# A graph layer's edge loop rebuilt: tiles of 128 edges, one f32 product per tile, bias moved into the node table, a ring of 26 row tiles

## The reference

```python
xn  = layernorm(x)                                    # 1250 x 512
msg = relu(xn[src] + edge_attr @ W_e + b_e)           # 21250 x 512
aggr = segment_sum(msg, dst, 1250)                    # summed by destination
h = (1 + eps) * xn + aggr
h = silu(batchnorm(h @ W1 + b1)); y = silu(batchnorm(h @ W2 + b2))
x = x + y                                             # then layernorm, top-k, experts
```

## Time and profile before

| | us |
|---|---|
| median of the three timed runs | 633.88 |
| span of the profiled execution, first to last instruction | 659.6 |
| first gather issued | 26.95 |
| last gather issued | 300.38 |
| last sum added to `aggT` (edge loop done) | 328.56 |
| expert stage begins (PE dense) | about 505 |

### The profile page before, as it was taken

One profiled execution on the slowest core, in us unless ns is written; L12 is line 12 of the kernel. 1 busy time (PEld: TensorE's weight loads), 2 busy tenths in 40 slices (PEclk: granted clock), 3 DMA queues, 4 the chain that ended last, 5 costly groups with the idle time before them and its releaser, 6 DMA issues.

```text
span 659.6 us, 12121 instructions
## 1 busy us (share of the span) xinstructions
PE 515.8 (78%) x4075; PEld 368.6 (56%) x4075; DVE 410.4 (62%) x1056; ACT 362.9 (55%) x754; POOL 304.4 (46%) x249
## 2 busy tenths in 40 slices
PE   3458678887868987978799996670279999999990
PEld 2324334554434553545445653550179999999990
DVE  7557676764554665766557963668666766766530
ACT  3527667654553555656648613843306667667760
POOL 3377887878777666772000000000054465555531
PEclk9979988997897988999989998785559999999996
DMA  9799866667766666663346730781027999994322
GB/s 240 221 227 208 206 177 181 181 185 188 183 187 176 162 160 163 174 176 98 118 139 233 186 120 0 218 286 63 0 60 232 280 293 283 283 280 82 59 32 28
DMA packets 76088, 111.59 MB, mean 169 GB/s; under 512 B 32201, under 2 KB 36865, under 8 KB 76027
## 3 DMA queue, kind: packets, MB, share of 16 engines
q0 software_dynamic: 43712, 53.95, 33.7%
q1 hardware_dynamic: 32211, 56.70, 28.5%
q10 hardware_dynamic: 104, 0.17, 0.1%
HBM read 97.81 MB, written 12.79 MB: 168 GB/s over the span
## 4 chain that ended last, share of the span: by engine, by line
PE 58%; issue 11%; DVE 11%; ACT 10%; DMA 4%; another core or an unknown queue 2%; POOL 1%; DVEq 1%; ACTq 1%; POOLq 0%; SPq 0%
PE bank L1365 19%; PE bank L1549 11%; PE bank L1342 10%; ACT big L612 4%; PE bank L1356 3%; DVE bank L995 3%; PE bank L1358 3%; PE bank L1575 2%; DMA big<-node_rows,edge_home 2%; PE bank L1412 1%; PE bank L1539 1%; PE bank L1530 1%; DVE rows_z L1172 1%; PE bank L1418 1%
## 5 line engine op out<-in xcount | busy, mean ns | idle before, releaser
L1342 PE MATMUL bank<-big,edge_home 125*64 125x256 f32 x688 | 99.0, 421 | 49.9 <-ACT big L612 34.1
L477 POOL DMA_INDIRECT big<-node_rows,edge_home x90 | 111.9, 1244 | 54.9 <-issue 47.7
L487 POOL DMA_INDIRECT big<-token_rows,idx x32 | 36.6, 1143 | 215.3 <-DVE idx L1230 209.8
L477 POOL DMA_INDIRECT pair<-node_rows,edge_home x80 | 99.4, 1243 | 29.3 <-issue 22.6
L612 ACT ACTIVATE big<-bank 125x512 f32<-125x512 f32 x170 | 96.0, 594 | 30.1 <-DVE bank L995 22.9
L1365 PE MATMUL bank<-big,pair 128*128 128x156 f16 (+2 forms) x1056 | 106.5, 260 | 1.1 <-DVE big L1050 0.9
L1342 PEld LDWEIGHTS bank<-big,edge_home 125*64 125x64 f32 x688 | 46.5, 146 | 92.2 <-ACT big L612 47.1
L1365 PEld LDWEIGHTS bank<-big,pair 128*128 128x128 f16 x1056 | 80.9, 97 | 24.6 <-issue 1.4
L1356 PE MATMUL bank<-edge_home 128*125 128x512 f16 x172 | 71.4, 415 | 6.0 <-issue 6.0
L995 DVE SCALAR_TENSOR_TENSOR bank<-big,bank 125x512 f32<-125x512 f32 x90 | 59.1, 708 | 26.7 <-PE bank L1358 14.2
L496 POOL DMA_INDIRECT out<-rows_z,idx x32 | 51.1, 1598 | 45.1 <-issue 26.1
(11 more groups left out here) (246 smaller groups left out, 915.4 us busy)
## 6 DMA issues: line engine op xcount, KB each, us to landing
raw<-in_L_ffn_w SPq DMA_DIRECT2D x12, 1024.0 KB, 5.5
edge_home<-in_L_ffn_w SPq DMA_DIRECT2D x6, 1024.0 KB
pair<-in_L_ffn_w SPq DMA_DIRECT2D x6, 1024.0 KB
pair<-in_edge_attr SPq DMA_DIRECT2D x36, 140.0 KB
xs_home<-in_x SPq DMA_DIRECT2D x10, 448.0 KB
xs_home<-in_L_ffn_w SPq DMA_DIRECT2D x4, 1024.0 KB
aggT<-in_L_ffn_w SPq DMA_DIRECT2D x4, 1024.0 KB
node_rows<-rows_z SPq DMA_DIRECT2D x5, 448.0 KB
```

The costliest lines, as they stand in the source:

```text
L477: pool.indirect_dma_start(row(i % RING, j), None, node_rows, bass.IndirectOffsetOnAxis(src_i[:, i, j:j + 1], 0)).then_inc(row_in[i % RING] ...
L487: pool.indirect_dma_start(xg[e % XR][:, a, :], None, token_rows, bass.IndirectOffsetOnAxis(idx[:, e, a:a + 1], 0)).then_inc(xg_in[e % XR], 16)
L1342: last = pe.matmul(bank[6 + b][a * WIN:(a + 1) * WIN, 0:H // 2], onehot[b][:, j, :], msg[:, b * J + j, a * (H // 2):(a + 1) * (H // 2)], s ...
```

## The change

The edge loop is rewritten; everything behind it stays.

- Tiles hold 128 edges: 167 tiles, 34 steps of five tiles, the last with two. The attributes arrive already turned, two tiles one above the other in the 128 partitions (64 attributes each), in 17 loads of five such pairs into three buffers. The lists of source and destination come in lane order.
- The product is one f32 matmul per tile (`edge_pair`): the even tile uses partitions 0 to 63 and the odd one 64 to 127 of both operands. The rounding, the turns and the copies of attributes go.
- Four PSUM banks hold products (`PB`); PE works two pairs ahead. `part_product` has two banks of its own.
- The bias is added to the normalised rows by DVE (`table(g)`) before they go to `node_rows`; SP waits for that instead of for ACT.
- Rows lie in a ring of 26 tiles, freed one at a time; POOL still waits once per step.
- The one-hot matrix is made by one instruction a step. The order on PE goes tile by tile: `fold(t)`, after every odd tile the pair two ahead.
- DVE's constants for the expert selection are made behind the second batch norm instead of ahead of the loop.

The core of the diff:

```diff
-                sp.wait_ge(xn_ready, (g + 1) * XG)
+                sp.wait_ge(tab_ready, g + 1)
                 for r0, r1 in SPRAY:
                     sp.dma_start(by_tile(node_rows)[r0:r1, g * XG:(g + 1) * XG, :],
-                                 xn[r0:r1, g * XG:(g + 1) * XG, :]).then_inc(tab_out, 16)
-            load_edges(1)
+                                 xs[r0:r1, g * XG:(g + 1) * XG, :]).then_inc(tab_out, 16)
+            for u in range(1, AR):
+                load_attr(u)
...
                 for i in range(SB):
-                    ago = RING if i >= SB % RING else SB % RING
-                    pool.wait_ge(row_used, w * (SB * J) + (CREDIT + (i - ago + 1) * J))
+                    pool.wait_ge(row_used, 1 + w * T + freed(tiles_of(i)[-1], RR))
...
+            def table(g):
+                dve.wait_ge(be_in, 32)
+                dve.wait_ge(xn_ready, (g + 1) * XG)
+                dve.tensor_tensor(xs[:, g * XG:(g + 1) * XG, :], xn[:, g * XG:(g + 1) * XG, :],
+                                  be_all.unsqueeze(1).to_broadcast([P, XG, H]), ALU.add).then_inc(tab_ready, 1)
...
+            norm_terms(2)
+            table(1)
...
+            statistics(3)
...
+            norm_terms(3)
+            table(2)
...
+            statistics(4)
+            norm_terms(4)
+            table(3)
...
+            table(4)
...
             def step(w, i):                                   # ACT
-                sum_copy(n, 1 - b)
-                for j in range(J):
-                    if j == 1 and i >= ZHEAD:
-                        part_copy(w, i - ZHEAD, b)
-                    if j == 3:
-                        act.wait_ge(edge_tr, n + 3)
-                        edge_columns(1 - b)
...
+                for j, t in enumerate(tiles_of(i)):
+                    act.wait_ge(row_used, 1 + w * T + t + 1)
+                    act.wait_ge(folded, 1 + w * T + freed(t, MR))
+                    act.activation(msg[:, t % MR, :], bank[t % PB][0:Q, :], ACT.Relu).then_inc(msg_ready, 1)
+                    if j == 1 and i >= 1:
+                        sum_copy(w, i - 1)
+                    if j == min(3, last) and i >= ZHEAD:
+                        part_copy(w, i - ZHEAD)
...
             def step(w, i):                                   # DVE
+                for j, t in enumerate(tiles_of(i)):
+                    dve.wait_ge(edge_ps, w * T + t + 1)
+                    dve.wait_ge(row_in[t % RR], row_landed(w, t))
+                    dve.tensor_tensor(bank[t % PB][0:Q, :], row(t), bank[t % PB][0:Q, :], ALU.add).then_inc(row_used, 1)
+                    if j == 1 and i + 1 < SB:
+                        columns_hot(w, i + 1)
+                    if j == min(3, last) and i >= 1:
+                        accumulate(w, i - 1)
...
+            def edge_pair(w, q):                              # PE
+                u, c = divmod(q, J)
+                if c == 0:
+                    pe.wait_ge(attr_in[u % AR], attr_landed(w, u))
+                for r, t in enumerate(range(2 * q, min(2 * q + 2, T))):
+                    side = slice(r * ED, (r + 1) * ED)
+                    pe.matmul(bank[t % PB][0:Q, :], attr[u % AR][side, c, :], We32[side, :],
+                              start=True, stop=True).then_inc(edge_ps, 1)
...
             def step(w, i):                                   # PE
+                for j, t in enumerate(tiles_of(i)):
+                    pe.wait_ge(msg_ready, 1 + w * T + t + 1)
+                    if j == 0:
+                        pe.wait_ge(acc_done, 1 + w * SB + max(0, i - 1))
+                    fold(t, j, last, b)
+                    if t % 2 == 1 and t // 2 + AHEAD < NP:
+                        edge_pair(w, t // 2 + AHEAD)
+                    if j == 1 and i >= 1:
+                        turn_sum(w, i - 1)
+                    if j == min(2, last) and i >= ZHEAD:
+                        part_product(w, i - ZHEAD)
```

More of the change, by code:

```diff
@@ L88, in gnn_ffn_kernel, with tiles_of, uses, row_landed @@
         token_rows = nc.dram_tensor("token_rows", (N, H), F32).ap()
[L90 to L104, removed]
+        def tiles_of(i):
+            return range(i * J, min((i + 1) * J, T))
+        def uses(slot, ring, n):
+            return len(range(slot, n, ring))
+        def row_landed(w, t):
+            return w * (16 * uses(t % RR, RR, T)) + (t // RR * 16 + 16)
+        def attr_landed(w, u):
+            return w * (16 * uses(u % AR, AR, NU)) + (u // AR * 16 + 16)
+        def freed(t, ring):
+            return max(0, t - ring + 1)
         xs_home = sb("xs_home", [128, NT * H], F32)
@@ L1289, in _ @@
         def _(pe):
-            pe.wait_ge(consts, 5)
-            for n, (i, bk) in enumerate(((1, bank[5]), (0, bank[2]))):
-                pe.wait_ge(ends_f_ready, n + 1)
-                for j in range(J):
-                    last = pe.transpose(bk[0:P, j * SB:(j + 1) * SB],
-                                        ends_f[i].rearrange("s (p j) -> s j p", j=J)[:, j, :], ident[0:SB, 0:SB])
-                last.then_inc(ends_ps, 1)
+            pe.wait_ge(consts, 3)
             pe.wait_ge(base_ready, 3)
-            pe.matmul(bank[3][0:P, 0:SB], ones[0:SB, 0:P], sb_diag[:], start=True, stop=True).then_inc(base_ps, 1)
+            pe.matmul(bank[3][0:Q, 0:SB], ones[0:SB, 0:Q], sb_diag[:], start=True, stop=True).then_inc(base_ps, 1)
             def node_transposes(t):
@@ L1310, in _ @@
                 node_transposes(t)
[L1311 to L1325 removed]
+            pe.wait_ge(base_ready, 7)
+            pe.matmul(bank[3][0:1, 64:65], ones[0:Q, 0:1], n_out[:], start=True, stop=True).then_inc(base_ps, 1)
             for t in range(2, NT):
@@ L1392, in step @@
-                for j in range(3):
-                    fold(j, b)
-                pe.wait_ge(edge_cp, n + 2)
-                for j in range(2):
-                    edge_product(j, 1 - b)
-            pe.wait_ge(edge_cp, 1)
-            for j in range(2):
-                edge_product(j, 0)
+                b, last = i % 2, len(tiles_of(i)) - 1
+                if i == 0:
+                    pe.wait_ge(msg_ready, 1 + w * T)
+                    for q in range(AHEAD):
+                        edge_pair(w, q)
```

447 lines of the change are left out of this document (180 added, 267 removed).

## The result

The changed kernel takes 646.21 us, the median of five runs (643.31 to 647.99), against 634.18 beside it: ratio 1.0188, 95% interval 1.0162 to 1.0214, or 12.0 us slower. The forecast was 639 and slower, so the sign is right and the size is not: +5 was expected. The profiled execution of the changed kernel has a span of 641.5 us and a time of 643.31, the quickest of the five. A second profile of the kernel before, taken for this part, has a span of 630.3 and a time of 632.18; it is the one to compare with, and the difference of these two spans is 11.2.

What follows compares the result with a forecast made beforehand. It took the gathers' pace to bound the loop, with compute close behind. First gather +8.3, gathers -3.7 and end after the last gather +0.4 made +5 on 633.9: 639, own range 635 to 645, outer range 614 to 662.

Steps and rivals of the forecast that it cites:

- The profile's 31 us: Edge loop before: about 31 us lost to PE's late signals in the profile, taken as mostly missing from timed runs.
- The rival that put them there: Edge loop: late signals also in timed runs, and the changed loop rides them out; 610 to 617, say 614; chance 0.20.
- Prologue: Ahead of the loop: DVE's table additions form a serial line, 4.7 us a group; first gather at 35.3, 8.3 later.
- Gathers: POOL in the loop: 167 gathers of 128 rows, 1.549 us apart, 258.7 in all, 3.7 less; they set the pace.
- Compute, the step that failed: Loop steps: PE needs 5.9 us, a step takes 7.4, just under the gathers' 7.75; 8.5 for steps 4 to 7.
- the upper end of 9.0: Loop step: longest time considered, with the four-bank ring at 4.75 us per five tiles and everything else queued into it.
- The 3 us that the forecast gave to the steps with a split: Loop steps 4 to 7 and three later ones: they fall behind the gathers and recover slowly, 3 us at the end.
- Row halves: PE's product pairs in the loop: two tiles on row halves run side by side, 2 x 0.43 us a pair.
- rival 4: PE's product pairs: row halves run one after the other, a pair takes 1.7 us; time 681; chance 0.10.
- Rival 3: PE in the loop: four more tiling changes a step cost about 0.17 us each; time 650 to 657; chance 0.10.
- Ring of 26 and moved constants: Row ring and DVE's expert constants: the longer ring gives nothing; the constants, about 3 us, cost nothing behind batch norm 2.
- The sum: Whole kernel: +8.3 first gather, -3.7 gathers, +0.4 end after the last gather; together +5, 639 us.

Runs made afterwards that it cites:

- fewer groups: Changed kernel with turn and part product issued in one group behind a pair, only in steps that have a part product: 641.92 us, ratio 1.0120.
- the version with both and all other edits: Changed kernel with early credit, sooner loads, four banks for node transposes, `W1` split ahead of the loop, late grouping and five banks: 613.11 us, ratio 0.9676.

## Why the prediction was right and wrong

- *The profile's 31 us*. Right: they were not in the timed runs, and 300 for the loop's end was 300.5 (328.1 in the first profile, so 27.6 were lost up to there). The rival that put them there (faster, 614) is refuted.
- *Prologue.* The additions of the table start at 12.41, 17.10, 21.61, 26.31 and 28.14, and the last ends at 29.37, as worked out. But the first gather was not at 35.3: it came at 39.45, against 26.95 before, since the credit of DVE had moved behind the node columns, a line of the change that I priced at nothing. With the credit where it was, it comes at 36.03. And +8.3 on the first gather was not the right term for the loop. In the kernel before, the loop's first addition is at 39.5, and its third then waits until 44.3 for rows that share the DMA engines with `W1`'s load. So 12.5 later at the gather became 3.1 later at the first sum.
- *Gathers.* Wrong: 1.549 was taken for 128 rows by adding 2 ns a row to the earlier trace rows, and they start 1.25 apart. A gather of 128 rows is cheaper than the 1.14 of one of 78, so no price by the row fits. This removes the pace on which the forecast was built. The page "DMA: Bandwidth & Descriptors" of the Trainium skill, section "Why a DMA increments its semaphore by 16 and not by 1", says that a DMA runs on the largest number of DMA engines up to 16 that divides the slowest dimension of both its access patterns, except for some direct copies; worked out by that rule it is 16 for 128 rows and 5 for 125. The traces agree in the direction: a gather of 128 rows lands 3.7 to 3.9 us after issue (median), one of 125 takes 5.7 to 5.8; the number of engines is in no view here, so that this is the reason is not shown.
- *Compute, the step that failed.* I took 7.4 a step and 8.5 for steps 4 to 7, from the kernel before, whose five tiles of a step go through five banks, one each; the ring of four stood only in the upper end of 9.0. Measured: 10.05 for each of steps 4 to 7, and 7.6 in steps with a part product (7.0 and 8.2 in turn). Five banks bring the four steps back to 8.2 and the others to 7.3, so the bank ring is the cause, and the lower clock behind its longer pauses is the larger part of its price in the four steps: at clock 1.00 a step with the split takes 8.7, near the 8.5 that I took. So the missing term is the clock, some 5.4 us, with the ring behind it. The 3 us that the forecast gave to the steps with a split were 7.1 in four of them, and steps 10 to 31 lost 2.6 more.
- *Row halves.* Right: a pair takes 1.06 with its change of tiling, side by side like the fold halves of the earlier trace rows; rival 4, with 1.7, is refuted, although 1.06 lies just above the 1.0 and 1.05 that I had named as limits. PE's need was mis-sized all the same: 5.9 a step held no price for a change of tiling, which is 0.10 to 0.15 for each of some eight groups and brings it to 6.7 to 7.1. Rival 3 had the mechanism and a price near it (0.17). Against the kernel before as it was, the loss went away in full without touching the number of groups. But against the kernel before with gathers of 128 rows, steps 10 to 31 lose 10.7 (171.2 against 160.5); fewer groups give 2.5 of that back, five banks 5.4, and the version with both and all other edits 14.2. So in these steps rival 3 is a part of the price, which dear gathers had hidden in the kernel before.
- *Ring of 26 and moved constants.* Right: nothing from the first, and 1.0 behind the loop, within what profiles differ there.
- *The sum.* Two errors hid each other. With 125 rows, where a gather is as dear as I thought, the kernel takes 656.5, 22 more than before, not 5; some 3 of that are its three more tiles. So the other terms were short by some 14, and the cheaper gather gave back some 7. That the time fell inside the forecast's outer range of 614 to 662 is in part this luck.

Not settled is what makes the clock fall: pauses of 2.87 and of 1.80 us were followed by the lower level in the changed kernel, and pauses of 1.80 and 2.38 with five banks were not.

## What to carry to other kernels

Count the buffers of the ring that a loop turns in, before and after: here a ring that is one shorter cost 0.3 us in a step without a long pause, and 1.9 in one with a pause, by the estimate above most of it through the lower clock behind it. Follow initial credits and increments of semaphores through a diff like instructions, since they are queued behind whatever their engine does first. When a gather's row count changes, measure the new count before scaling a price by rows: 128 rows were cheaper than 125 and than 78; which other counts are, no run here shows. And when one limit goes (here the gathers), compare again with a kernel before that has lost it too.

## What the runs showed of the hardware

- An indirect gather of 128 rows of 2 KB costs POOL 0.97 to 0.99 us and one of 125 rows 1.23 to 1.25, in both kernels; 170 and 167 gathers of 128 go with 19,232 and 18,992 packets on the software queue, 170 of 125 with 43,712.
- After a pause of 2.87 us PE ran its next products at the lower level (2.08 for a pair, not 1.13) for some 9.6 us, up to 91.0. A pause of 1.80 was followed by it too (111.30 in the changed kernel), and pauses of 1.80 and 2.38 were not (79.70 and 87.34 with five banks).
- Each group of matmuls with another tiling cost PE about 0.1 to 0.15 us that matmuls of the same tiling do not.
